# Inverse softmax sums applied to the transposed attention output instead of the probabilities, in the first attention layer of a two-layer decoder

## What is computed

```
x = x + L0_attn(layernorm(x))

q, k, v = split(layernorm(x) @ weight_qkv.T)      # 16 heads of 32; 4 k and v heads, each for 4 q heads
scores  = q @ k.T / sqrt(32);  causal mask to -inf
probs   = softmax(scores)
out     = (probs @ v) @ weight_proj.T
```

## Time and profile before

| | |
|---|---|
| median of three executions | 4074.44 us |
| profiled execution | 4052.58 us |
| its span, first to last instruction | 4050.8 us |
| mean granted TensorE clock over the span | 0.938 |
| PE busy | 3502.1 us (86%) |
| DVE busy | 2477.1 us (61%) |
| ACT busy | 1643.1 us (41%) |
| POOL busy | 896.6 us (22%) |
| loop of `first_layer`, first `tops` to the last `round_back` | 42.06 to 348.4 us |

### The profile page before, as it was taken

The page is one execution under the profiler, slowest core; times in us unless marked ns, Lnnn a source line. Parts: engine busy times, 40 slices in busy tenths (PEclk is TensorE's granted clock), DMA queues, the critical chain, the costliest instruction groups (busy, mean ns, idle before and its releaser), DMA issues. The chain is left out here.

```text
span 4050.8 us, 55081 instructions
## 1 busy us (share of the span) xinstructions
PE 3502.1 (86%) x18156; PEld 2769.7 (68%) x18156; DVE 2477.1 (61%) x6496; ACT 1643.1 (41%) x3680; POOL 896.6 (22%) x965
## 2 busy tenths in 40 slices
PE   6881898699599999959999987999689979997999
PEld 4550776577377777747777766888567756665887
DVE  4884786688466666656666657899655552225533
ACT  5552443444333333334343433788233433332222
POOL 3561343244122222112222223000421210000000
PEclk9875999899799999989999998999889989998999
DMA  4004000100200000020000006999510004332000
GB/s 159 14 14 122 0 0 1 62 0 0 89 19 25 19 25 19 8 90 26 19 25 19 25 0 213 360 401 404 182 57 1 1 27 128 114 108 100 28 9 19
DMA packets 86514, 296.70 MB, mean 73 GB/s; under 512 B 9104, under 2 KB 15248, under 8 KB 81120
## 3 DMA queue, kind: packets, MB, share of 16 engines
q1 hardware_dynamic: 79968, 276.45, 19.1%
q0 software_dynamic: 6400, 18.36, 1.5%
HBM read 252.57 MB, written 42.21 MB: 73 GB/s over the span
## 5 line engine op out<-in xcount | busy, mean ns | idle before, releaser
L39 PE MATMUL bank<-cross_w,cross_ctx_part 128*125 128x512 f32 x2304 | 594.1, 409 | 12.6 <-DVE cross_qn L883 8.0
L39 PEld LDWEIGHTS bank<-cross_w,cross_ctx_part 128*125 128x125 f32 x2304 | 425.8, 186 | 134.7 <-issue 8.9
L39 PE MATMUL bank<-self_w,self_xq 128*112 128x512 f32 x1024 | 268.3, 411 | 94.5 <-ACT self_xq L780 94.5
L889 DVE TENSOR_REDUCE cross_neg_max<-bank 112x1 f32<-112x375 f32 x256 | 133.2, 530 | 295.8 <-PE bank L699 292.9
L815 ACT ACTIVATE cross_prob<-bank,cross_neg_max 112x375 f32<-112x375 f32 x256 | 147.5, 576 | 323.0 <-DVE cross_neg_max L889 323.0
L39 PEld LDWEIGHTS bank<-self_w,self_xq 128*112 128x112 f32 x1024 | 177.4, 181 | 146.4 <-ACT self_xq L780 95.3
L39 PE MATMUL bank<-moe_wt,moe_zT 128*128 128x448 f32 x1176 | 265.9, 375 | 2.1 <-DVE moe_zT L1460 1.5
L1455 DVE TENSOR_TENSOR moe_wt<-moe_raw,moe_wt 128x1792 fp32r<-128x1792 f32 (+1 forms) x111 | 231.6, 2109 | 13.5 <-ACT moe_wt L1362 10.5
L39 PEld LDWEIGHTS bank<-moe_wt,moe_zT 128*128 128x128 f32 x1176 | 215.9, 190 | 18.2 <-issue 1.7
L39 PE MATMUL bank<-mlp_zT,mlp_signs 128*128 128x448 f32 x1024 | 220.9, 369 | 4.7 <-DVE mlp_zT L2069 4.7
L616 POOL TENSOR_TENSOR cross_ve<-cross_mv,eps 125x4 f32<-125x4 f32 (+1 forms) x160 | 31.7, 198 | 871.5 <-DVE cross_mv L874 871.5
(11 more groups left out here) (387 smaller groups left out, 7679.6 us busy)
## 6 DMA issues: line engine op xcount, KB each, us to landing
moe_raw<-in_moe_w SPq DMA_DIRECT2D x74, 896.0 KB, 7.4
moe_raw<-in_moe_w SPq DMA_DIRECT2D x37, 1024.0 KB, 8.5
stream<-in_L1f SPq DMA_DIRECT2D x32, 768.0 KB, 4.4
cross_ctx_raw<-in_ctxT SPq DMA_DIRECT2D x32, 750.0 KB, 4.2
wide_ctxT<-in_ctxT SPq DMA_DIRECT2D x16, 750.0 KB, 12.6
wide_ctx_rows<-in_ctx SPq DMA_DIRECT2D x16, 750.0 KB
expert_rows<-a_zeros SPq DMA_DIRECT2D x1, 8960.0 KB, 26.5
moe_zrow<-expert_rows SPq DMA_DIRECT2D x35, 256.0 KB, 7.7
```

Source lines behind the costliest of these rows:

```text
L39: mm = pe.matmul(out, a, b, start=first and n == 0, stop=last and n == len(pairs) - 1)
L889: dve.tensor_reduce(neg_max[:, HS * t:HS * (t + 1)], score_bank(t)[0:S, 0:HS * NK].rearrange("p (h n) -> p h n", h=HS), AX.X, ALU.max, neg ...
```

## The change

The sums are inverted once a tile, spread to 32 equal copies each (128 x 512), turned by four matmuls against the identity so that they stand as the output stands, copied out of PSUM and multiplied into the transposed output. POOL's divides go, and the probabilities are transposed as the exponentials leave them. `clip` and `shift` now stand together ahead of the one `invert`; `scale_out` stands between `round_back` and `z_low`. `out_high` and `out_low` read the scaled output in SBUF. Bank 6 now serves the spread too, which brings waits on `spread_taken`.

```diff
-            def divide(t, r):
-                pool.wait_ge(s["inverse_ready"], 2 * t + r // 2 + 1)
-                pool.tensor_tensor(prob[:, r], prob[:, r], inverse[:, r, :, None].to_broadcast([T, 4, T]), ALU.mult)\
-                    .then_inc(s["probs_ready"], 1)
             for t in range(NT):
-                for r in range(4):
-                    divide(t, r)
...
             def transpose_q(t):
                 pe.wait_ge(s["q_taken"], t + 1)
-                wait(pe, s["z2T_taken"], t - 3)
+                wait(pe, s["spread_taken"], t - 1)
...
             def transpose_probs(t, rows):
                 for r in rows:
-                    pe.wait_ge(s["probs_ready"], 4 * t + r + 1)
+                    pe.wait_ge(s["exp_done"], 4 * t + r + 1)
...
+            def spread_inverse(t):
+                pe.wait_ge(s["inverse_ready"], t + 1)
+                wait(pe, s["z2T_taken"], t - 1)
+                for c in range(4):
+                    mm = pe.matmul(tiled(6)[:, c, :], inverse[:, c, :], k.ident[:],
+                                   start=True, stop=True)
+                mm.then_inc(s["inverse_in_psum"], 1)
+
             def transpose_z2(t):
...
+                pe.wait_ge(s["spread_taken"], min(t + 2, NT))
...
                 weigh_values(t)
+                spread_inverse(t)
                 if t + 2 < NT:
                     transpose_z(t + 2)
...
+            def take_spread(t):
+                act.wait_ge(s["inverse_in_psum"], t + 1)
+                wait(act, s["out_scaled"], t)
+                act.activation(spread[:], tiled(6), ACT.Copy).then_inc(s["spread_taken"], 1)
+
             def out_high(t):
-                act.wait_ge(s["outT_in_psum"], t + 1)
-                act.activation(oT[0][:], tiled(7), ACT.Copy).then_inc(s["out_high"], 1)
+                act.wait_ge(s["out_scaled"], t + 1)
+                act.activation(oT[0][:], out[:], ACT.Copy).then_inc(s["out_high"], 1)
...
                 for r in range(1, 4):
                     take_probsT(t, r)
+                take_spread(t)
                 if t + 2 < NT:
                     z_high(t + 2)
...
             def out_low(t):
                 dve.wait_ge(s["out_high"], t + 1)
-                dve.tensor_tensor(oT[1][:], tiled(7), oT[0][:].bitcast(F32), ALU.subtract).then_inc(s["out_low"], 1)
-
-            def invert(t, r):
-                dve.wait_ge(s["exp_done"], 4 * t + r + 2)
-                dve.reciprocal(inverse[:, r:r + 2], total[:, r:r + 2]).then_inc(s["inverse_ready"], 1)
+                dve.tensor_tensor(oT[1][:], out[:], oT[0][:].bitcast(F32), ALU.subtract).then_inc(s["out_low"], 1)
+
+            def invert(t):
+                dve.wait_ge(s["exp_done"], 4 * t + 4)
+                dve.reciprocal(inverse[:].rearrange("p c (r d) -> p c r d", d=32),
+                               total[:].rearrange("p r c -> p c r")[:, :, :, None].to_broadcast([T, 4, 4, 32]))                    .then_inc(s["inverse_ready"], 1)
+
+            def scale_out(t):
+                dve.wait_ge(s["outT_in_psum"], t + 1)
+                wait(dve, s["out_low"], t)
+                dve.wait_ge(s["spread_taken"], t + 1)
+                dve.tensor_tensor(out[:], tiled(7), spread[:], ALU.mult).then_inc(s["out_scaled"], 1)
...
                     normalise_again(t - 2)
-                invert(t, 0)
                 if t >= 3:
                     clip(t - 3)
-                invert(t, 2)
-                if t >= 3:
                     shift(t - 3)
+                invert(t)
                 if t:
                     add_out(t - 1)
                     measure_rows(t - 1)
                 if t >= 3:
                     round_back(t - 3)
+                scale_out(t)
                 if t + 2 < NT:
                     z_low(t + 2)
```

More of the change, by code:

```diff
@@ L2234, in first_layer @@
              "qT_in_psum", "kT_in_psum", "q_ready", "k_ready", "scores_in_psum", "minus_max", "exp_done",
-             "inverse_ready", "probs_ready", "probsT_in_psum", "probsT_ready", "outT_in_psum", "out_high",
+             "inverse_ready", "inverse_in_psum", "spread_taken", "out_scaled", "probsT_in_psum", "probsT_ready", "outT_in_psum", "out_high",
              "out_low", "y_in_psum", "x_done", "x_stored", "cleared", "stat1", "centre1", "vareps1", "rooted1", "z1_ready",
@@ L2252, in first_layer @@
         total = sb("total", [T, 4, 4])
-        inverse = sb("inverse", [T, 4, 4])
+        inverse = sb("inverse", [T, 4, P])
+        out = sb("out", [P, DC, T])
+        spread = sb("spread", [P, DC, T])
         oT = [sb(f"oT{i}", [P, DC, T], F32R) for i in range(2)]
```

## The result

The changed kernel takes 4084.19 us (median of seven, 4075.37 to 4089.63), the kernel before 4070.09 on the same chip: ratio 1.0031, 95% interval 1.0019 to 1.0043. The forecast, no change, was wrong. The time, 4084, lies above the forecast's own range of 4066 to 4083 and within the wide one of 4061 to 4091. It lies there by luck: that range reached so far up for a dearer reciprocal (rival B), which did not come. On another chip the same two kernels gave 1.0048 (1.0034 to 1.0061).

The account below looks back on a forecast made before the run. It took the layer to be a loop of waits through POOL's divides, with no engine full. Terms -1.3 + 1.2 + 1.7 - 4.0 + 0 + 2.3 = -0.1 us gave 4074 us, own range 4066 to 4083, 8 in 10 within 4061 to 4091.

Parts of the forecast that it names:

- rival B: At invert, between shift and add_out: a dearer reciprocal, 3.9 to 4.9 us, makes DVE the bound; +8 to +21 us; chance 0.23.
- What bounds the kernel, what goes: Full loop, tiles 3 on: no engine full, a loop of waits; 56 POOL divides and 28 small reciprocals go.
- the idle 3.07 us before z_low: DVE, between round-back and z_low: 3.07 us of waiting for z_high, to pay for DVE's added work.
- The reciprocal: On DVE, one 128x512 reciprocal a tile, taken as 3.28 us from the slope of smaller sizes.
- Rivals A: On DVE, long reciprocals stream at 0.68 us; mean period 17.7, total 4046 us; chance 0.1.
- DVE's new chain: DVE's instruction starts from one tops to the next: invert at 9.29, period 19.54 us if DVE never waits.
- What becomes late next: PE behind add_out: weigh_values from 13.25, then spread, z_high, z_low, tops; 20.10 us at the low clock.
- The wait for x_done: On PE, weigh_values waits for add_out because bank 7 still holds the previous tile's y; x_done at 13.2.
- Tiles 3 to 11: Nine full loop tiles: period 19.8, low clock in about half of them; -4.0 us together.
- the two levels that the working gave: Loop period: 19.54 us by DVE's chain at full clock, 20.10 by PE's way at low clock.
- The other tiles: Outside tiles 3 to 11: tile 0 -1.3, tile 1 +1.2, tile 2 +1.7, tile 12 0, tile 13 +2.3 us, tail 0.

Follow-up runs that it names:

- once out_low is repaired: Changed kernel with scale_out writing back into bank 7, so out_high and out_low read PSUM as before the change: 4064.09 us, ratio 1.0028.
- With both terms repaired: Changed kernel with out scaled in bank 7 and the spread issued as four transposes: 4059.07 us, ratio 1.0005 to the kernel before.
- the two single repairs: Changed kernel with only out scaled in bank 7: 4064.09 us, ratio 1.0028; with only the spread issued as transposes: 4083.8 us, ratio 1.0029.

## Why the prediction was wrong, step by step

- **What bounds the kernel, what goes:** right. Expo and magic are 0.69 in the loop, POOL has only scale_rows and the powers, and the idle 3.07 us before z_low did pay for the reciprocal: the reciprocal added to the kernel before shows it.
- **The reciprocal:** right, 3.35 for 3.28 us, 6.3 ns an element. Rivals A and B fell with it (B had the sign, by a price that is not there), and so did the reading of the repeat count that the Trainium skill gives (VectorE: DVE Perf Modes, First, the fixed hardware budget) as eight cycles an element.
- **DVE's new chain, "tops and out_low 2.99" and "normalise, normalise_again and clip 2.63":** the step that failed. I took both from before. The diff moves out_low's first operand from PSUM to SBUF, and with two SBUF inputs it waits for scale_rows. Measured 4.76 (185.37 less 180.61) and 1.63: together +0.77, so the reciprocal starts at T = 10.05 and not 9.29, and weigh_values behind add_out at 14.00 and not 13.25. Normalise is then no longer held, which is why only 0.77 of out_low's 1.76 counts. The Trainium skill (SBUF — State Buffer, Who interferes with whom) says that a VectorE instruction with two SBUF inputs contends with a GpSimd one that reads SBUF; the 2.44 against 0.68 us agree. The Trainium skill says there too that one with at most one SBUF input does not contend, unless it runs in a mode that uses both ports. The reciprocal agrees, 3.35 us beside scale_rows and without it; normalise, whose only tensor input is x, took 1.58 us beside scale_rows and 0.53 behind it, and no run shows in which mode it ran.
- **What becomes late next, "four fp32 128x128 matmuls, priced as transpose_z":** failed too. An fp32 matmul that is no transpose runs as two records, as the row of weigh_values with eight for four showed already. In tiles 3 to 11 the spread took 1.60 to 1.87 us to the next start for 0.91. The wait for x_done was placed right (13.27 for 13.25, once out_low is repaired).
- **The two together in one tile.** The forecast's PE way was 13.25 + 2.0 + 0.91 + 1.11 + 0.63 + 2.20 = 20.10. In tile 7 of the changed kernel the same terms measure 14.00 + 0.99 + 1.63 + 1.10 + 0.63 + 2.20 = 20.55, its period. The 2.0 for weigh_values was too much in this tile, since the clock fell only behind it, and hides a part of the two misses.
- **Tiles 3 to 11:** forecast 19.8, measured mean 20.92. With both terms repaired it is 19.73, near the two levels that the working gave. In the slow ones weigh_values needs 1.86 for 2.0, and tops come 2.3 to 2.6 behind z_low for 2.20. In the loop the repairs give back 16.6 us, all that the changed kernel lost.
- **The other tiles:** tile 1 right (+1.4 for +1.2), tile 2 +2.4 for +1.7. Tile 0 wrong: +0.3 for -1.3. I had weigh_values at full clock there, but it ran at half, as it had before, and the spread behind it in eight records. Tile 12 +1.2 for 0. Tile 13 +4.8 for +2.3: out_low waits there in full, with no normalise behind it to take its share of the wait, and scale_out waits 0.97 for the spread. Tail +0.4.
- **Sum of the parts of the loop:** +0.3 + 1.4 + 2.4 + 6.1 + 1.2 + 4.8 + 0.4 = +16.6 us, which is 0.4% of 4070; the timed ratios, 1.0031 and 1.0048, stand on either side of it.

What stays open: the timed ratios of the two single repairs (1.0028, 1.0029) lie within the noise of that of the changed kernel, so their 9 and 7 us rest on one profiled execution each, and two profiles of the changed kernel itself differ by 1.3 us in the loop; only the pair is shown by timing. How much of what a repair gives back comes from a higher granted clock is not separated.

## What to carry to other kernels

When a diff moves an operand from PSUM to SBUF, price again every instruction that reads it: the same subtraction went from 0.68 to 2.44 us because of what POOL did beside it. Count the records of a matmul's own kind, transposes and products apart. An operation that costs by the element belongs ahead of a broadcast and not behind it: 16 reciprocals a row and a copy on an idle engine did the work of 512, and turned 0.3 to 0.5% of loss into 0.7% of gain together with the two repairs.

## What the runs showed of the hardware

A reciprocal of 128x512 takes 3.35 us on DVE, 128x16 takes 0.25; a multiplication of 128x512 takes 0.69. The reciprocal does not wait for a POOL instruction that reads SBUF, as operations with two inputs in SBUF did here: scale_rows ran beside it in its usual 3.61 us. The round-back, begun 0.33 us after scale_rows, stood still until that was over. Four fp32 products of 128x128 are eight records and need 0.99 to 1.00 us to the next start at a granted clock of 1.00 and 1.87 at 0.50; issued as transposes they are four records and need 0.49 and 0.91.
